# Products with V in fewer, larger groups, five turning places for the probabilities, and the column sums in another place of TensorE's order

## The reference

```python
    qkv = encodings @ W_attn + b_attn
    ...
    scores = jnp.einsum('bhki,bhqi->bhkq', k, q) / math.sqrt(HEAD)     # 16 heads of 32
    mask = jnp.arange(n)[:, None] <= jnp.arange(n)[None, :]
    scores = jnp.where(mask, scores, jnp.float32(-10000.0))
    attn = jax.nn.softmax(scores, axis=2)
    combined = jnp.einsum('bhkq,bhkl->bhql', attn, v)
    ...
    return out @ W_out + b_out
...
    # then: top 512 of 1024 tokens by a router score, gelu MLP 512 -> 2048 -> 512, scatter back
x = _layernorm(x + attention(x)); x = _layernorm(x + ffn(x))
```

## Time and profile before

| | before |
|---|---|
| median of 3 runs | 2496.51 us (2496.45 to 2498.16) |
| the profiled execution | 2497.64 us |
| its span in the trace | 2495.8 us |
| PE busy | 2437.9 us (98% of the span) |
| POOL busy | 1566.2 us (63%) |
| DVE busy | 1677.7 us (67%) |
| ACT busy | 1227.0 us (49%) |
| PE granted clock, mean | 0.993 of full |

### The profile page before, as it was taken

One profiled execution on the slowest core, in us unless ns is written; L12 is line 12 of the kernel. 1 busy time (PEld: TensorE's weight loads), 2 busy tenths in 40 slices (PEclk: granted clock), 3 DMA queues, 4 the chain that ended last, 5 costly groups with the idle time before them and its releaser, 6 DMA issues.

```text
span 2495.8 us, 40908 instructions
## 1 busy us (share of the span) xinstructions
PE 2437.9 (98%) x14104; PEld 1798.0 (72%) x14104; DVE 1677.7 (67%) x4384; ACT 1227.0 (49%) x2211; POOL 1566.2 (63%) x1481
## 2 busy tenths in 40 slices
PE   8999999999999999999999999998999999999997
PEld 6666676777677767676767667763788888888886
DVE  6767778778777777777888787775755544553533
ACT  3665566666566666666666666666531111111110
POOL 2877888788877888877888888885323132221311
PEclk9999999999999999999999999998999999999999
DMA  4233445335344444534434354343421011010100
GB/s 178 95 128 117 161 138 199 129 124 187 136 146 162 145 145 141 175 133 166 157 129 161 125 180 145 128 162 97 169 64 43 19 34 33 26 34 26 32 20 17
DMA packets 167649, 287.72 MB, mean 115 GB/s; under 512 B 23258, under 2 KB 58138, under 8 KB 166172
## 3 DMA queue, kind: packets, MB, share of 16 engines
q1 hardware_dynamic: 160276, 268.26, 31.1%
q0 software_dynamic: 7168, 16.85, 2.1%
HBM read 117.23 MB, written 65.11 MB: 73 GB/s over the span
## 4 chain that ended last, share of the span: by engine, by line
PE 83%; POOL 11%; DVE 2%; issue 1%; ACT 1%; DMA 0%; SPq 0%; POOLq 0%; DVEq 0%; ACTq 0%
PE PS L1623 14%; PE PS L1602 14%; PE PS L1464 11%; POOL Pa L902 10%; PE PS L1549 10%; PE PS L1515 9%; PE PS L1567 9%; PE PS L1472 8%; PE PS L1477 6%; PE PS L1484 2%; POOL Pm L858 1%; PE PS L1439 1%; PE PS L1583 0%; DVE nm L1130 0%; DVE xTl L1223 0%
## 5 line engine op out<-in xcount | busy, mean ns | idle before, releaser
L902 POOL TENSOR_TENSOR Pa<-Pa,Pm 128x512 f32<-128x512 f32 (+1 forms) x602 | 751.9, 1271 | 129.3 <-ACT Pm L1012 106.7
L1549 PE MATMUL PS<-Qp,Kp 128*128 128x512 f32 (+3 forms) x1536 | 491.0, 355 | 8.7 <-ACT Pm L1012 4.1
L1515 PE MATMUL PS<-Kp,Qp 128*128 128x512 f32 (+3 forms) x1536 | 485.3, 351 | 6.6 <-DVE nm L1130 5.5
L1012 ACT ACTIVATE Pm<-PS 128x512 f32<-128x512 f32 (+1 forms) x643 | 358.3, 568 | 243.7 <-PE PS L1549 194.0
L1130 DVE TENSOR_REDUCE nm<-PS 128x1 f32<-128x512 f32 x512 | 344.7, 687 | 157.2 <-PE PS L1515 156.9
L902 POOL TENSOR_TENSOR Pa<-Pa,P 128x512 f32<-128x512 f32 (+1 forms) x297 | 371.9, 1274 | 64.7 <-ACT P L1012 53.6
L1515 PEld LDWEIGHTS PS<-Kp,Qp 128*128 128x128 f32 x1536 | 276.2, 189 | 105.4 <-issue 41.6
L974 ACT ACTIVATE G<-PS,b1c 128x512 f32<-128x512 f32 x128 | 88.2, 689 | 536.5 <-PE PS L1602 520.3
L1549 PEld LDWEIGHTS PS<-Qp,Kp 128*128 128x128 f32 x1536 | 274.8, 189 | 93.5 <-ACT Pa L1012 29.0
L1138 DVE CUSTOM_DVE_ANT_0 PS<-PS,maskA 128x384 f32<-128x384 f32 (+3 forms) x512 | 246.3, 509 | 121.9 <-PE PS L1515 119.9
L1623 PE MATMUL PS<-W2h,Gs 128*128 128x512 f32 x1024 | 316.6, 390 | 1.1 <-DVE W2l L1228 1.1
(11 more groups left out here) (154 smaller groups left out, 4261.2 us busy)
## 6 DMA issues: line engine op xcount, KB each, us to landing
Qp<-nat SPq DMA_DIRECT2D x192, 256.0 KB, 2.5
Kp<-nat SPq DMA_DIRECT2D x192, 256.0 KB, 2.9
o_s<-Of SPq DMA_DIRECT2D x64, 256.0 KB, 2.1
xb<-in_x SPq DMA_DIRECT2D x64, 256.0 KB, 3.4
Ot<-o_s SPq DMA_DIRECT2D x64, 256.0 KB, 3.0
h_s<-hs SPq DMA_DIRECT2D x64, 256.0 KB, 2.1
out<-xb SPq DMA_DIRECT2D x64, 256.0 KB, 2.2
x_raw<-in_xt SPq DMA_DIRECT2D x15, 1024.0 KB, 6.4
```

The lines of the kernel that those rows point to most:

```text
L902: e.tensor_tensor(to, to, probs(u, k)[:, h0:h0 + many, 0:w], ALU.add).then_inc(s["padd"], many)
L1012: e.activation(probs(u, k)[:, hh[0]:hh[-1] + 1, 0:w], tile_bank(j)[:, 0:len(hh) * w].rearrange("p (h n) -> p h n", n=w), ACT.Exp).then_inc ...
L1515: ins = e.matmul(to, Qp[:, u % 4, h_, qt * P:qt * P + P], Kp[:, (2 * i + k0 // 512) % 4, h_, 0:w], start=True, stop=True)
L1549: ins = e.matmul(tile_bank(j)[:, x_ * w:x_ * w + w], Kp[:, (2 * i + k // 4) % 4, h_, k % 4 * P:k % 4 * P + P], Qp[:, u % 4, h_, 512 - w:51 ...
```

## The change

Products with V come in one group in a narrow unit, steps 0 to 3, and in three in a wide unit, steps 0-1, 2-3 and 4-7. All follow two beats after their last step is formed; the last group of a wide unit stands in the beat of its job N. N moves one beat earlier (14 in place of 15) and behind the products of its beat. The probabilities of a pair go through five places, a to e, whose names change from pair to pair; the two narrowest steps of a unit share one place. POOL's additions are not taken when a step is formed but by a small schedule of their own (`sums`), in which an addition of a unit starts a beat after its step 0 is multiplied, and the masks (`keep`) go between additions. One of the two bias additions moves from beat 27 to beat 8.

```diff
-PRODUCTS = (((0,), (1, 2, 3)), ((0,), (1, 2), (3, 4), (5, 6, 7)))
-PV_LAG = ((1, 2), (2, 2, 3, 3))
+PRODUCTS = (((0, 1, 2, 3),), ((0, 1), (2, 3), (4, 5, 6, 7)))
+PV_LAG = 2
+IN_SUMS = 1
+PLACES = "abccdebcaebb"
+TURN = {"a": "c", "b": "a", "c": "e", "d": "d", "e": "b"}
+KEEP_BEATS, ADD_BEATS, EXP_BEATS = 0.39, {512: 0.78, 384: 0.62, 256: 0.78, 128: 0.78}, 0.6
...
-        return 15
+        return 14
...
-                n = self.formed[u, k1] + PV_LAG[u % 2][j]
+                n = self.formed[u, k1] + PV_LAG
+                if u % 2 and j == 2 and not by_products(u):
+                    n = max(n, self.beat["N", u - 1 if j == 0 else u])
...
+    def sums(self):
+
+        self.adding = {}
+        keeps = [(u, k) for u in range(U) for k in range(ksteps(u)) if diag(u, k) is not None]
+        pieces = [(u, k, h0) for u in range(U) for k in range(1, ksteps(u)) if not by_products(u) and not in_sums(u, k)
+                  for h0 in range(0, HG, many_heads(width(u, k)))]
+        t = float(self.first)
+        while keeps or pieces:
+            at_keep = self.formed[keeps[0]] + EXP_BEATS + (2 if keeps[0][1] == 0 else 0) if keeps else 1e9
+            at_add = 1e9
+            if pieces:
+                u, k, h0 = pieces[0]
+                if (u, k) not in keeps:
+                    at_add = max(self.formed[u, k] + EXP_BEATS, self.multiplied[u, 0] + 1)
+            t = max(t, min(at_keep, at_add))
+            if at_keep <= t:
+                self.adding.setdefault(int(t), []).append((keeps.pop(0), None))
+                t += KEEP_BEATS
+            else:
+                self.adding.setdefault(int(t), []).append(((u, k), h0))
+                pieces.pop(0)
+                t += ADD_BEATS[width(u, k)]
...
-            if k == 0:
-                return acc[:, u % 2, :, :]
-            a = added(u, k) % 3
-            return Pm[:, a, :, :] if a < 2 else P3[:, :, :]
+            to = {"a": acc[:, 0, :, :], "b": Pm[:, 0, :, :], "c": Pm[:, 1, :, :], "d": acc[:, 1, :, :],
+                  "e": P3[:, :, :]}[place_of(u, k)]
+            return to[:, :, 256:512] if k == ksteps(u) - 1 else to
...
-                n = T.beat[j] - (3 if T.beat[j] % (2 * BEATS) > BEATS else 15)
-                if T.beat[j] % BEATS != 14 or n < load + 4:
+                n = load + 3 if T.beat[j] % (2 * BEATS) > BEATS else T.beat[j] - 15
+                if T.beat[j] % BEATS != 14 or n < load + 3:
...
-                todo += [(1, 2, x_) for x_ in T.pieces[n] if x_[0][0] == "N"]
+                todo += [(3, 2, x_) for x_ in T.pieces[n] if x_[0][0] == "N"]
                 todo += [(2, 3, x_) for x_ in T.pv_steps(n)]
```

More of the change, by code:

```diff
@@ L98, in in_sums, with place_of, occupants, many_heads @@
 def in_sums(u, k):
-    return u % 2 == 1 and k == ksteps(u) - 1
+    return u % 2 == 1 and k >= ksteps(u) - IN_SUMS
 def additions(a):
-    return a - a // 10
+    return (10 - IN_SUMS) * (a // 10) + min(a % 10, 10 - IN_SUMS)
+def place_of(u, k):
+    name = PLACES[4 * (u % 2) + k]
+    for _ in range(u // 2):
+        name = TURN[name]
+    return name
+def occupants(u, k):
+    if k == ksteps(u) - 1:
+        return []
+    steps = [(x_, y_) for x_ in range(max(0, u - 3), u + 1) for y_ in range(ksteps(x_)) if (x_, y_) < (u, k)]
+    last = [x_ for x_ in steps if place_of(*x_) == place_of(u, k)][-1:]
+    return [x_ for x_ in steps if last and x_[0] == last[0][0] and place_of(*x_) == place_of(u, k)
+            and (x_ == last[0] or x_[1] == last[0][1] - 1 == ksteps(x_[0]) - 2)]
+def many_heads(w):
+    return 1 if w > 256 else 2 if w > P else HG
 def by_products(u):
@@ L116, in diag @@
     return 4 * u + i if i >= 0 else None
-def kept_early(u, k):
-    return not by_products(u) and k >= 2 and diag(u, k - 1) is not None and k < ksteps(u)
 def width(u, k):
@@ L206, in __init__ @@
         self.streams()
+        self.sums()
         self.nat, self.packs, self.freed = {}, {}, {}
@@ L251, in streams @@
     def streams(self):
-        self.tiles, self.formed, self.products = {}, {}, {}
+        self.tiles, self.formed, self.products, self.multiplied = {}, {}, {}, {}
         ring = []
@@ L880, in gpsimd @@
                         layer_norm(o_number(j))
-                for u, k in T.steps_formed(n):
-                    i = diag(u, k)
-                    if i is not None and not kept_early(u, k):
+                for (u, k), h0 in T.adding.get(n, ()):
+                    if h0 is None:
                         keep(u, k)
[L885 to L888, removed]
+                        continue
+                    a, w = added(u, k), width(u, k)
+                    if h0 == 0:
+                        if diag(u, k) is not None:
+                            e.wait_ge(s["keep"], diag(u, k) + 1)
                         else:
@@ L893, in gpsimd @@
                             e.wait_ge(s["pv"], ksteps_before(u) + 1)
[L894 to L903, removed]
+                    many = many_heads(w)
+                    to = probs(u, 0)[:, h0:h0 + many, 512 - w:512]
+                    e.tensor_tensor(to, to, probs(u, k)[:, h0:h0 + many, 0:w], ALU.add).then_inc(s["padd"], many)
                 for j in o_add.get(n, ()):
@@ L997, in scalar @@
                     if hh[0] == 0:
[L998 to L1008, removed]
+                        for u0, k0 in occupants(u, k):
+                            if by_products(u0) and k0 < ksteps(u0) - 1:
+                                e.wait_ge(s["p_sum"], k0 + 1 + (ksteps(U - 2) - 1) * (u0 % 2))
+                            elif by_products(u0) or k0 == 0 or in_sums(u0, k0):
                                 e.wait_ge(*done(("N", u0)))
                             else:
-                                e.wait_ge(s["p_sum"], k0 + 1 + (ksteps(U - 2) - 1) * (u0 % 2))
+                                e.wait_ge(s["pv"], ksteps_before(u0) + k0 + 1)
+                                e.wait_ge(s["padd"], 4 * additions(added(u0, k0) + 1))
                     e.activation(probs(u, k)[:, hh[0]:hh[-1] + 1, 0:w],
@@ L1483, in dense @@
                         for h_ in range(4):
-                            ins = e.matmul(to[32 * h_:32 * h_ + 32, :], one32, acc[:, u % 2, h_, :], start=True,
+                            ins = e.matmul(to[32 * h_:32 * h_ + 32, :], one32, probs(u, 0)[:, h_, :], start=True,
                                            stop=u % 2 == 0)
-                        if u % 2:
-                            ins = sums(u, ksteps(u) - 1)
+                        for k_ in range(ksteps(u)):
+                            if in_sums(u, k_):
+                                ins = sums(u, k_)
                 elif kind == "T":
```

1 line of the change is left out of this document (added).

## The result

The changed kernel takes 2648.5 us (median of 4 runs, 2644.6 to 2652.0) against 2496.7 for the kernel before: ratio 1.060, 95% interval 1.059 to 1.062, slower. The prediction said 2625 in a range of 2545 to 2665, slower with 0.91. The profiled execution has a span of 2642.8 us.

The account below looks back on a forecast made before the run. TensorE, busy 98%, bounds the kernel before; afterwards POOL's additions set each pair. Over 31 pairs +88 us, plus 40 for the slow clock, on 2497.64 gave 2626, taken as 2625 us; range 2545 to 2665.

Parts of the forecast that it names:

- The mechanism: Likeliest case: wide sums wait for POOL's additions, then TensorE's clock slows; 2590 to 2660 us, chance 0.62.
- The wait: TensorE at the wide unit's sums, waiting for POOL's last addition: 3.5 us a pair (2.2 to 4).
- The chain: POOL's serial additions from the wide step 0's product to the wide sums: 32.2 us.
- late exponentials: Delay in POOL's additions where masks of steps 4 and 5 await ACT: 1.0 us, then about 0.3.
- TensorE's work in the same stretch: TensorE's instructions between the wide step 0's product and the wide sums: 28.7 us with small stalls.
- A steady pair without a slow clock: One narrow and one wide unit in the attention, clock term excluded: from 52.7 to 55.9 us.
- Saved by one block: Five blocks of products with V a pair instead of six, saving TensorE's way in and out: -0.33 us.
- the stall ahead of the transposition: Two 384-column score tiles waiting for banks ACT had not read; expected to vanish, -0.4 us a pair.
- +0.5 behind the sums: TensorE waiting for score banks while ACT does Ln and Exp first: +0.5 us a pair (0.2 to 0.8).
- The clock: TensorE at 1.2 GHz for 3.4 us after each pause: 1.3 us a pair (0 to 1.7), 40 us in all.
- The sum: Whole kernel: +88 us over 31 pairs and 40 us for the slow clock, +128 us.
- the last of the 31 pairs: Final pair of the attention, priced like any other steady one: 55.9 us plus 1.3 for the slow clock.

Follow-up runs that it names:

- sums_3: Changed kernel with IN_SUMS = 3, so TensorE's sums take steps 5 and 6 of the wide unit instead of POOL's additions; 2547.7 us, ratio 1.020.
- both0_early: Changed kernel with step 0 of the wide and of the narrow unit each multiplied alone and earlier, six blocks a pair; 2535.3 us, ratio 1.015.
- filled_wait: Changed kernel with ten unneeded 128x512 products ahead of TensorE's wait for a wide unit's additions; 2624.1 us, ratio 1.051.

## Why the prediction was right, step by step

**The mechanism** was right: the chain of additions between the wide unit's step 0 and its sums had 1.5 us to spare, the change cut TensorE's work between these two ends, and the rest of the chain became a wait. Moving either end, shortening it and lengthening it moved the time in the direction expected each time; the amounts were off where the clock or the schedule's order changed too. That the blocks or the places make the sums wait is excluded by `sums_3`, in which the waits vanish with both in place, and spoken against by `both0_early`. Not all of the time came back with the waits: 38 us are left in `both0_early` and 50 in `sums_3`, of which the added sums are 34 by my count (31 x 1.09).

**The wait**: 3.5 us were forecast (2.2 to 4), 2.8 measured in most steady pairs (1.0 to 1.7 in four, and 3.6 to 4.5 in the first four), 91 us in all. The chain was forecast at 32.2 from the product's end to the sums, with 1.3 for late exponentials; measured are 31.9 (538.6 to 570.47), with 1.46 for late exponentials. TensorE's work in the same stretch was forecast at 28.7 and took 29.1 (538.6 to 567.7). Both sizes were near, and their errors add to the 0.7 by which the wait is shorter. One step of the working does not come out: exponentials 1.5 us behind a tile at 12.4 end at 13.9 and not at 14.2, a wait of 0.6 for step 4 and not of 1.0; measured are 0.91. The sum's 30.5 for the instructions themselves was a little high: without its waits the chain now lasts 30.0, where that pair of before took 30.54.

**A steady pair without a slow clock**: 55.9 forecast; 55.7 in `filled_wait`, where the same wait is filled, and 55.6 to 55.8 in the five pairs of after with hardly any slow clock.

**Saved by one block**: -0.33, and -0.4 for the stall ahead of the transposition, against +0.5 behind the sums: -0.23 net forecast, -0.35 measured between the two kernels without additions. The stall did not vanish but moved to the first score tile behind the transposition, since ACT does Ln and Exp of the sums first.

**The clock**: forecast 40 us. Between the first and the last transposition of wide units, 144.5 us more are 87 more of the sums' waits (90.9 less 3.8), 6.6 which the kernels without additions also differ by between the same two transpositions (1619.8 against 1613.2), and a remainder of 51. That remainder is no measurement of the clock; 109 us more at half speed bound it at 55 from above, `filled_wait` at 24 from below. The sum is near, but its parts are not what was forecast, and that is luck: the prediction had one slow stretch behind every pause, 3.4 us for 1.3. Here some steady pairs have 6.8 us for some 2.3, others next to nothing.

**The sum** was 128 and the measured difference 152. The 26 pairs between the first four and the last were forecast at 1459 and 26 x 1.3 for the clock, 1493, and took 1499; inside them errors cancel, since five of those with loads took 59.2 to 61.5 for 58.0 and a part of the steady ones 55.6 to 55.8 for 57.2. The first four took 225 for 217 + 5, with waits of 3.6 to 4.5 us. The term that was clearly too small is the last of the 31 pairs, which I had priced like any other: it took 63.6 for 57.2, with a wait of 7.3 us. Some 3 us lie outside the pairs, where I had left start and end "as they are". The remaining 5 are between this profiled execution (span +147.0) and the medians. The range's upper end does not come out of its terms either: 31 x (4 + 0.8 + 1.7 - 0.73) is 179, so 2676 and not 2665; the measured time lies inside both.

## What to carry to other kernels

When products are grouped to save a fixed cost of the engine that is busy all the time, look at what the first and the last product of each group release. An engine at 60% may hold a serial chain between them that has only a microsecond to spare. Read the chain as one duration against the work that the other engine has between the same two points; its share over the pair does not show this. And a pause of TensorE of 2.8 us can cost more than its length: in most pairs here its clock fell behind it, and a pair with 6.8 us at half clock was some 2.3 us longer.

## What the hardware showed beyond that

The kernel before loses 32 us to POOL's additions although TensorE waits only 3.8 us for them: without them it takes 2463.6 against 2495.6 beside it. In the pairs with the loads of a new sequence, DVE subtracts one tensor in SBUF from another (xTl). Its instructions of before and of before without additions, with the shortest, median and longest duration in ns:

```profile
L1223 DVE TENSOR_TENSOR xTl<-x_raw,xTh x64: 676/1104/1829, 6.0 to 1472.7; 128x512 fp32r<-128x512 f32 x64
```

```profile
L1223 DVE TENSOR_TENSOR xTl<-x_raw,xTh x64: 680/683/783, 5.5 to 1450.5; 128x512 fp32r<-128x512 f32 x64
```

Beside POOL's additions they take 1104 ns in the middle, without them 683. POOL pays too; in such a pair of before four additions read

```profile
612.39 6.49 POOL L902 TENSOR_TENSOR Pa<-Pa,Pm 128x512 f32<-128x512 f32 x4
```

1.62 us each in place of 1.27. The Trainium skill ("SBUF — State Buffer", "Who interferes with whom") says that a DVE instruction with two inputs in SBUF contends with a GpSimd instruction that reads SBUF, over a pair of ports that only one of them can hold. The rows agree that each is slower beside the other. Taken from narrow unit to narrow unit, five of the pairs with loads last 54.4 to 54.7 us with the additions and 52.7 to 52.9 without. From 300 us on, the seven pairs that grow by over 1 us make 11 of the 32 us. That the contention makes these pairs longer fits, but other work of the same pairs was not tested apart. Of the rest, 11 lie in the first four pairs (201.8 against 191.0) and 8 in the last (55.5 against 48.0); why there is not shown.
